# A fused attention and butterfly-FFN kernel: the first unit's row maxima made in two halves, and sixteen extra matmuls in the head

## Chip, cores and metric

One NeuronCore of a Trainium2 chip. The metric is the device time of one execution in microseconds, as the median of several runs. The engines are TensorE (PE; its weight loads are shown as PEld), VectorE (DVE), ScalarE (ACT), GpSimd (POOL) and SyncE (SP), which here issues every DMA.

## What is computed

One post-norm transformer layer in float32. x is 4 x 1024 x 128; there are 16 heads of 64.

```python
q, k, v = (einsum('BSE,EHK->BSHK', x, w) for w in (w_q, w_k, w_v))
logits = einsum('BSHK,BMHK->BSHM', q, k) / sqrt(64)
probs = softmax(logits + causal_mask, axis=3)
att = einsum('BSHK,EHK->BSE', einsum('BSHM,BMHK->BSHK', probs, v), w_o)
x = layernorm(x + att)
h = butterfly(x @ W_exp + b_exp, up_weights)            # 9 stages over 512 features
y = butterfly(gelu(h + up_bias), down_weights) @ W_con + b_con + down_bias
x = layernorm(x + y)
```

The softmax subtracts each row's maximum, so a query row's maximum over its keys must be known before its probabilities are made.

## The kernel before

**Units, steps, places.** The attention is cut into 32 units, one for each batch and pair of heads (`UNITS`). A unit has 1024 queries in two chunks of 512 and 1024 keys in tiles of 128. `STEPS` lists its 12 steps (query chunk, key tile) under the causal mask: steps 0 to 3 are chunk 0 with tiles 0 to 3, steps 4 to 11 chunk 1 with tiles 0 to 7. `window(u)` on TensorE runs the steps in order. In each, `scores` makes two products for each of the two heads, one of the high parts of Q and K (L692) and one of `KH1` by `QL` (L696). `QL` has the low part of Q in its first 64 partitions and, in partition 64, the row of negated maxima, which meets a one in `KH1`: the maximum is subtracted by the matmul. `fill` puts other work ("fillers") at three places of a step: BETWEEN the heads, BEHIND the second head and LATE, which is behind the probability-value products (`pv`, L717). Those run in blocks: behind step 1 the last five of the unit before, behind step 8 those of steps 0 to 3, behind step 9 those of steps 4 to 6.

**Fillers.** `FILL` lists them by step and place. They work for the next unit: the four projections `("proj", n, c)` (n 0 is Q, n 1 is K; c the chunk of tokens), the two V pieces, and the 21 maxima `MAXES` (L631). A maximum multiplies 128 queries of one head by up to 512 keys and VectorE reduces the product (`tensor_tensor_reduce` with the mask at L991, `tensor_reduce` at L994). The first six of `MAXES` are all of query chunk 0 (`CHUNK0_MAXES`); the other 15 are chunk 1. Each filler writes one of four PSUM banks (`WORK`), in turn, and waits until the filler four before it has been read.

**Behind a projection.** ScalarE copies the high part out (L797, two instructions), VectorE subtracts for the low part (L929, two instructions), and SP copies halves between partitions (`copies`, L396 for Q, L400 for K). The first maximum of each chunk waits for both projections' splits and for the copies.

**Behind the last maximum.** In `consume`, VectorE reduces and negates (`NEGM`, L998) and transposes it in four instructions (`NROW`, L1004); SP moves the row into `QL` (`rows`, L408), and the first L696 product of the unit waits for it (`m_landed`).

**The head.** Before unit 0, `PREFETCH` runs for it: projections, V pieces, all 21 maxima, and the first projection of unit 1. Meanwhile GpSimd sends the bias row through the butterfly (L190, L192, L494); for the last two stages it needs a transfer of SP's (L429, `BROW`). Then it starts on masks (L504) and on the sums of probabilities (L518 to L528). SP works through one written order: inputs, `copies(0)`, the loads of w_o, W_con and the biases, `BROW`, W_exp and the next tokens, `rows(0)`, and then for each unit `copies(u + 1)` and `rows(u + 1)`. Every wait in it holds what is behind.

**Weights of the next units.** `stage_low` (Q and K weights) and `stage_v_low` (V weights) on VectorE subtract high parts, both inputs in SBUF (L929, WST and WSV).

Of the kernel before, what the change touches and what calls it, by code (L numbers as in the profile page):

```python
# [24 lines left out]
F32 = mybir.dt.float32  # L25
# [22 lines left out]
NS = len(STEPS)  # L48
# [53 lines left out]
FILLERS = [(s, place, f) for s in range(NS) for place in range(3) for f in FILL[s][place]]  # L102
EARLY = ("proj", 0, 0)
# [9 lines left out]
NWORK, BLK = 4, 32  # L113
LAY_UNITS = TILES // 2
# [15 lines left out]

def unit_fillers(u):

    b, n = u // PAIRS, u % PAIRS
    rows = []
    for s, place, f in FILLERS:
# [12 lines left out]
    rows += [(s, place, f) for f, (unit, s, place) in X1_AT.items() if unit == u]  # L148
    rows += [(s, place, f) for f, (unit, s, place) in ONCE_AT.items() if unit == u]
    if b < B - 1 and n < LAY_UNITS:  # L150
        rows.append(LAY_AT + (("lay", b + 1, n),))
    return sorted(rows, key=lambda row: row[:2])


PREFETCH = [("proj", 0, 0), ("v", 0), ("proj", 1, 0), ("proj", 0, 1), ("v", 1), ("proj", 1, 1)] + MAXES + [("proj", 0, 0)]
# [39 lines left out]
def post_norm_layer(nc, x, w_q, w_k, w_v, w_o, W_exp, b_exp, up_w, up_b, down_w, W_con, b_con, down_b, out):  # L195
    ctx = ExitStack()
    with ctx:
# [156 lines left out]

        block = ctx.enter_context(nc.Block())
# [3 lines left out]
        def _(sp):  # L359
# [42 lines left out]

            def rows(unit):

                par = unit % 2
                sp.wait_ge(nrow_made, (unit + 1))
                dst = QL[K:K + 1, par, :, :].rearrange("a h (t c) -> a (h t) c", t=TILES)
                sp.dma_start(dst.bitcast(F32), NROW[0:2 * TILES, :].bitcast(F32)).then_inc(m_landed, 16)  # L408
# [14 lines left out]
            sp.sem_inc(sums_landed, 16)  # L423
            sp.dma_start(wo_nat, w_o.rearrange("e h k -> e (h k)")).then_inc(in_wo, 16)
# [7 lines left out]
            rows(0)  # L432
# [14 lines left out]
            sp.wait_ge(m_landed, 16 * UNITS)  # L447
# [129 lines left out]
        def _(pe):  # L577
# [20 lines left out]
            def filler(u, f, at):  # L598
# [21 lines left out]
                elif f[0] == "max":  # L620
                    pieces = f[1]
                    unit, nxt = u + 1, (u + 1) % 2
# [60 lines left out]
            def scores(unit, s):  # L683
# [3 lines left out]
                for h in range(2):  # L687
# [6 lines left out]
                    if s == 0 and h == 0:  # L694
                        pe.wait_ge(m_landed, (unit + 1) * 16)
# [99 lines left out]
        def _(act):  # L795
# [123 lines left out]
        def _(dve):  # L919
# [40 lines left out]
            def consume(u, f, at):  # L960
# [19 lines left out]
                elif f[0] == "max":  # L980
                    pieces = f[1]
# [14 lines left out]
                    if f == MAXES[-1]:  # L996
# [191 lines left out]
```

## Time and profile before

| | |
|---|---|
| median of 3 runs | 1035.09 us (1034.93 to 1035.8) |
| the profiled execution | 1035.9 us, span 1034.2 us |
| TensorE busy | 1007.0 us (97% of the span) |
| VectorE, GpSimd, ScalarE busy | 778.0, 750.9, 613.1 us |
| mean granted clock of TensorE | 0.993 |
| first 26 us, first slice of 40 | PE 6 tenths, clock 8 tenths |

All times in the rows are microseconds from the start of the span, and durations are microseconds unless marked ns. A timeline row gives start, duration, engine, line, operation, output<-input, and shapes; "x4" is a group of four in a row, and the bracket at the end is the idle time before it and what ended it. A matmul's duration holds its way through the array; the distance between starts shows what it occupies. The granted clock is a share of 2.4 GHz.

### The profile page before, as it was taken

How to read it: one execution, taken by the hardware profiler on the slowest of the kernel's cores; microseconds unless marked ns; L12 is line 12 of the kernel's file. 1: busy time of each engine (PE TensorE's matmuls, PEld its weight loads, DVE VectorE, ACT ScalarE, POOL GpSimd, SP SyncE). 2: the span in 40 equal slices, each digit the busy share in tenths (PEclk: the TensorE clock that was granted, in tenths of full speed). 3: DMA queues.
4: the chain of work that ended last, by engine and by line, in shares of the span. 5: the costliest groups of instructions: out<-in, count | busy, mean ns of one | idle time of the engine just before them, and what ended most of it. 6: DMA issues, size and time to landing. Idle time of an engine off the chain costs nothing.

```text
span 1034.2 us, 17742 instructions
## 1 busy us (share of the span) xinstructions
PE 1007.0 (97%) x5816; PEld 697.7 (67%) x5816; DVE 778.0 (75%) x2112; ACT 613.1 (59%) x1246; POOL 750.9 (73%) x715
## 2 busy tenths in 40 slices
PE   6799999999999999999999999999999999999997
PEld 4566676676666776676666766767666766765687
DVE  7767777877777777878788778877778888785356
ACT  3555656566656656666556656666555656665544
POOL 6567887777768887777778877777778887777510
PEclk8899999999999999999999999999999999999999
DMA  6233122233222222232232222332222222320002
GB/s 190 62 83 82 45 72 53 62 83 83 58 68 62 63 65 60 63 83 63 70 76 58 62 56 55 83 83 63 66 60 74 63 57 57 83 64 22 22 11 73
DMA packets 48602, 68.71 MB, mean 66 GB/s; under 512 B 15191, under 2 KB 25083, under 8 KB 48510
## 3 DMA queue, kind: packets, MB, share of 16 engines
q1 hardware_dynamic: 48510, 67.57, 25.3%
q8 instruction: 47, 0.77, 0.3%
q14 instruction: 45, 0.37, 0.1%
HBM read 31.11 MB, written 2.36 MB: 32 GB/s over the span
## 4 chain that ended last, share of the span: by engine, by line
PE 92%; DVE 3%; DMA 2%; ACT 1%; issue 1%; POOL 0%; SPq 0%; POOLq 0%; ACTq 0%
PE O L717 25%; PE WORK L631 14%; PE SC L692 14%; PE SC L696 13%; PE WORK L644 6%; PE WORK L679 3%; PE WORK L607 3%; PE WORK L609 3%; PE WORK L608 3%; PE WORK L772 2%; PE WORK L617 1%; PE WORK L619 1%; PE WORK L618 1%; DVE WORK L991 1%; DMA R<-RROW 1%
## 5 line engine op out<-in xcount | busy, mean ns | idle before, releaser
L863 ACT ACTIVATE PR<-SC 128x512 f32<-128x512 f32 (+3 forms) x768 | 352.3, 490 | 263.9 <-PE SC L696 231.4
L519 POOL TENSOR_TENSOR SUM<-SUM,PR 128x1024 f32<-128x1024 f32 (+3 forms) x256 | 419.0, 1637 | 14.8 <-POOL SUM L528 0.5
L991 DVE CUSTOM_DVE_ANT_0 WORK<-WORK,CMASK 128x128 f32<-128x128 f32 (+3 forms) x512 | 239.3, 514 | 65.7 <-PE WORK L631 65.6
L692 PE MATMUL SC<-QH,KHL 128*128 128x512 f32 (+3 forms) x768 | 268.8, 356 | 3.1 <-ACT PR L863 3.0
L696 PE MATMUL SC<-QL,KH 128*128 128x512 f32 (+3 forms) x768 | 261.7, 346 | 3.3 <-DMA QL<-NROW 3.3
L504 POOL TENSOR_SCALAR_AFFINE_SELECT PR<-PR 128x256 f32<-128x256 f32 x256 | 105.9, 415 | 198.0 <-ACT PR L863 197.9
L631 PE MATMUL WORK<-KHL,QH 128*128 128x512 f32 (+3 forms) x768 | 226.5, 365 | 5.9 <-DMA KH<-KHL 4.1
L717 PE MATMUL O<-PR,VLO 128*64 128x512 f32 (+3 forms) x1024 | 200.0, 522 | 0.3 <-DVE OT L1075 0.3
L692 PEld LDWEIGHTS SC<-QH,KHL 128*128 128x128 f32 x768 | 145.2, 189 | 60.7 <-ACT PR L863 28.5
L631 PEld LDWEIGHTS WORK<-KHL,QH 128*128 128x128 f32 x768 | 136.7, 191 | 59.3 <-issue 35.4
L994 DVE TENSOR_REDUCE MP<-WORK 128x1 f32<-128x512 f32 x256 | 164.1, 684 | 4.8
L696 PEld LDWEIGHTS SC<-QL,KH 128*128 128x128 f32 x768 | 145.4, 189 | 14.2 <-DMA QL<-NROW 3.7
L929 DVE TENSOR_TENSOR QL<-WORK,QH 64x512 fp32r<-64x512 f32 x128 | 88.0, 687 | 86.7 <-ACT QH L797 85.5
L528 POOL TENSOR_TENSOR SUM<-PR 128x768 f32<-128x768 f32 x64 | 135.9, 2124 | 1.4 <-ACT PR L863 1.4
L717 PEld LDWEIGHTS O<-PR,VLO 128*64 128x64 f32 x1024 | 64.9, 136 | 104.4 <-issue 77.0
L929 DVE TENSOR_TENSOR KHL<-WORK,KHL 64x512 fp32r<-64x512 f32 x128 | 88.1, 689 | 34.2 <-ACT KHL L797 32.1
L797 ACT ACTIVATE QH<-WORK 64x512 fp32r<-64x512 f32 (+1 forms) x132 | 78.0, 591 | 26.2 <-PE WORK L609 22.6
L797 ACT ACTIVATE KHL<-WORK 64x512 fp32r<-64x512 f32 x128 | 75.7, 592 | 5.0 <-PE WORK L609 1.4
L717 PE MATMUL O<-PR,VHI 128*64 128x256 f32 (+3 forms) x512 | 74.3, 432 | 0.0
L991 DVE DVE_READ_ACCUMULATOR2_ANT MP<- 128x1 f32 x512 | 72.3, 141 | 0.0
L717 PEld LDWEIGHTS O<-PR,VHI 128*64 128x64 f32 x512 | 36.8, 137 | 52.6 <-issue 46.6
L644 PE MATMUL WORK<-WOT,OT 128*128 128x128 f32 x512 | 63.8, 278 | 0.6 <-DVE OT L1075 0.6
(132 smaller groups left out, 1099.0 us busy)
## 6 DMA issues: line engine op xcount, KB each, us to landing
QH<-QH SPq DMA_DIRECT2D x128, 128.0 KB, 2.4
KH<-KHL SPq DMA_DIRECT2D x128, 128.0 KB, 2.3
R<-RROW SPq DMA_DIRECT2D x64, 256.0 KB, 3.8
SW<-in_L_ffn_up_weights_dram SPq DMA_DIRECT2D x9, 512.0 KB, 4.4
SW<-_L_ffn_down_weights_dram SPq DMA_DIRECT2D x9, 512.0 KB, 4.3
out_dram<-X SPq DMA_DIRECT2D x7, 256.0 KB, 2.3
X<-in_L_attn_x_BSE_dram SPq DMA_DIRECT2D x3, 512.0 KB, 4.5
X<-in_L_attn_x_BSE_dram SPq DMA_DIRECT2D x2, 256.0 KB, 3.3
```

The lines of the kernel that those rows point to most:

```text
L519: nc.gpsimd.tensor_tensor(total, total, prob(unit, s), ALU.add).then_inc(add_done, 1)
L528: nc.gpsimd.tensor_tensor(total, first[:, :, START[s]:], prob(unit, s), ALU.add).then_inc(add_done, 1)
L631: t = nc.tensor.matmul(w[:, at_col:at_col + n], QH[:, nxt, h, qt * P:(qt + 1) * P], KHL[:, nxt, h, lo:lo + n], start=True, stop=True)
L644: t = nc.tensor.matmul(w[:, k * P:(k + 1) * P], attended(pair, qc)[:, k * P:(k + 1) * P], WOT[:, pair % PAIRS, :], start=pair < last, stop ...
L692: nc.tensor.matmul(dst, KHL[:, par, h, kt * P:(kt + 1) * P], QH[:, par, h, q0:q0 + n], start=True, stop=False)
L696: nc.tensor.matmul(dst, KH1[:, par, h, kt * P:(kt + 1) * P], QL[:, par, h, q0:q0 + n], start=False, stop=True).then_inc(scores_ready, 1)
L717: t = nc.tensor.matmul(O[qc][h * K:(h + 1) * K, START[s]:], values(unit, kt)[:, h * K:(h + 1) * K], p[:, h, :], start=kt == 0, stop=s == L ...
L797: return nc.scalar.activation(dst, src, ACT.Copy)
L863: nc.scalar.activation(prob(unit, s)[:, h, :], SC[use % NSC][:, 0:n], ACT.Exp, scale=K ** -0.5).then_inc(exp_done, 1)
L929: return nc.vector.tensor_tensor(dst, src, hi_part.bitcast(F32), ALU.subtract)
L991: op = nc.vector.tensor_tensor_reduce(cols, cols, CMASK[:, CH - n:], 1.0, LOWEST, ALU.add, ALU.max, cell)
L994: op = nc.vector.tensor_reduce(cell, cols, AX_X, ALU.max)
```

## The change

1. The head makes unit 0's maxima only up to the tenth: the six of chunk 0, and four of chunk 1 (`FIRST[6:10]`). The eleven others are fillers in steps 0 to 3 of unit 0. They need new lists for unit 0 (`FIRST_FILL`), in which unit 1's projections come in steps 3 and 4 and its maxima in steps 4 to 10 (now 1 to 9).
2. Unit 0's row is made and moved in two halves. Behind the sixth maximum VectorE reduces, negates and transposes once, behind the last a second time; SP moves each half in two transfers (`first_rows`). The first product of step 0 waits for the first half, that of step 4 for the second.
3. On SP `first_rows(0)` stands ahead of the loads of w_o, W_con and the biases; `first_rows(1)` stands where `rows(0)` was.
4. In `PREFETCH` the K projection comes ahead of the first V piece, and the second V piece comes behind the maxima. `stage_low(1)` moves behind the sixth maximum.
5. Sixteen matmuls of 512 columns (`keep_warm`) are added in the head, six behind the last projection and one behind each of ten maxima. They write a score bank that nobody reads.

```diff
+FIRST = [("first", i) for i in range(len(MAXES))]
+WARM_AFTER = {4: 6} | {n: 1 for n in range(5, 15)}
+FIRST_FILL[0] = [FIRST[10:11], FIRST[11:12], []]
+FIRST_FILL[1] = [FIRST[12:13], FIRST[13:15], []]
+FIRST_FILL[2] = [FIRST[15:16], FIRST[16:18], []]
+FIRST_FILL[3] = [FIRST[18:19], FIRST[19:21], [("proj", 1, 0), ("proj", 0, 1)]]
+FIRST_FILL[4] = [[("proj", 1, 1)], [], MAXES[0:1]]
+FIRST_FILL[5] = [[("v", 0)], MAXES[1:3], []]
+FIRST_FILL[6] = [MAXES[3:5], [], [("v", 1)] + MAXES[5:7]]
+FIRST_FILL[7] = [MAXES[7:9], [], MAXES[9:11]]
+FIRST_FILL[8] = [MAXES[11:13], [], MAXES[13:15]]
+FIRST_FILL[9] = [MAXES[15:17], MAXES[17:19], []]
+FIRST_FILL[10] = [MAXES[19:21], [("proj", 0, 0)], []]
...
-PREFETCH = [("proj", 0, 0), ("v", 0), ("proj", 1, 0), ("proj", 0, 1), ("v", 1), ("proj", 1, 1)] + MAXES + [("proj", 0, 0)]
+PREFETCH = [("proj", 0, 0), ("proj", 1, 0), ("v", 0), ("proj", 0, 1), ("proj", 1, 1)] + MAXES[:CHUNK0_MAXES]
+PREFETCH += FIRST[CHUNK0_MAXES:10] + [("v", 1), ("proj", 0, 0)]
...
+            def first_rows(c):
+
+                sp.wait_ge(nrow_made, c + 1)
+                for h in range(2):
+                    dst = QL[K:K + 1, 0, h, c * CH:(c + 1) * CH].rearrange("a (t c) -> a t c", t=TPC)
+                    row = h * TILES + c * TPC
+                    sp.dma_start(dst.bitcast(F32), NROW[row:row + TPC, :].bitcast(F32)).then_inc(m_landed, 16)
...
             copies(0)
             sp.sem_inc(sums_landed, 16)
+            first_rows(0)
             sp.dma_start(wo_nat, w_o.rearrange("e h k -> e (h k)")).then_inc(in_wo, 16)
...
-            rows(0)
+            first_rows(1)
...
-                    if s == 0 and h == 0:
-                        pe.wait_ge(m_landed, (unit + 1) * 16)
+                    if (unit, s, h) == (0, 0, 0):
+                        pe.wait_ge(m_landed, 32)
+                    elif (s, h) == (0, 0) or (unit, s, h) == (0, FIRST_OF[1], 0):
+                        pe.wait_ge(m_landed, rows_landed(unit))
...
+            def keep_warm(times):
+
+                for _ in range(times):
+                    nc.tensor.matmul(SC[0][:, :], XTH[:, 0:P], XTH[:, 0:CH], start=True, stop=True)
...
-                    if f == MAXES[-1]:
+                    if f == MAXES[-1] or (u < 0 and f == MAXES[CHUNK0_MAXES - 1]) or f == ("first", len(MAXES) - 1):
...
-                if f == LAST_PROJ:
+                if f == MAXES[CHUNK0_MAXES - 1]:
                     stage_low(1)
```

## Rows read from the trace of the kernel before

**Rows 1.** Windows: stretch, length, busy us of each engine (instructions), clock, DMA share, GB/s.
```profile
93.50:123.00 29.50, 29.44 (x171) 20.26 (x172) 21.80 (x61) 18.45 (x40) 23.10 (x22) 1.00 0.26 70
```

**Rows 2.** Windows of the head and of unit 0's start, same columns.
```profile
19.00:28.00 9.00, 8.97 (x18) 4.87 (x18) 9.00 (x30) 0.00 (x0) 5.55 (x5) 0.50 0.55 175
33.00:35.60 2.60, 2.60 (x6) 2.06 (x7) 0.00 (x0) 1.19 (x2) 0.24 (x1) 0.50 0.40 92
36.00:38.00 2.00, 1.94 (x10) 1.33 (x8) 0.88 (x2) 1.96 (x5) 0.00 (x0) 1.00 0.00 0
```

**Rows 3.** Timeline of TensorE, the first product with the row.
```profile
32.91 0.80 PE L696 MATMUL SC<-QL,KH 128*128 128x512 f32 x1 [3.26 <-DMA QL<-NROW]
```

**Rows 4.** Timeline of ScalarE, the first copy out of a projection.
```profile
9.19 1.19 ACT L797 ACTIVATE QH<-WORK 64x512 fp32r<-64x512 f32 x2 [1.09 <-PE WORK L609]
```

**Rows 5.** Timeline of VectorE, 15 to 31 us.
```profile
15.84 1.39 DVE L929 TENSOR_TENSOR KHL<-WORK,KHL 64x512 fp32r<-64x512 f32 x2
...
17.97 0.30 DVE L991 CUSTOM_DVE_ANT_0 WORK<-WORK,CMASK 128x128 f32<-128x128 f32 x1
...
21.52 0.33 DVE L991 CUSTOM_DVE_ANT_0 WORK<-WORK,CMASK 128x128 f32<-128x128 f32 x1
...
22.02 2.48 DVE L994 TENSOR_REDUCE MP<-WORK 128x1 f32<-128x512 f32 x4
...
29.96 0.19 DVE L998 TENSOR_REDUCE NEGM<-MP 128x16 f32<-128x32 f32 x1
```

**Rows 6.** Timeline of SP's queue: the first load, and the rows' issues.
```profile
17.05 0.51 SPq L424 DMA_DIRECT2D OT<-in_L_attn_w_o_dram  x1
...
31.05 0.56 SPq L408 DMA_DIRECT2D QL<-NROW  x1
...
37.10 1.10 SPq L400 DMA_DIRECT2D KH<-KHL  x2
...
59.78 0.55 SPq L408 DMA_DIRECT2D QL<-NROW  x1
```

**Rows 7.** Timeline of TensorE, unit 1's first maximum.
```profile
40.06 0.47 PE L631 MATMUL WORK<-KHL,QH 128*128 128x128 f32 x2 [2.12 <-DMA KH<-KHL]
```

**Rows 8.** Timeline of GpSimd, 22 to 51 us.
```profile
22.29 2.28 POOL L192 TENSOR_TENSOR SUM<-R,SUM 1x512 f32<-1x512 f32 x2 [4.04 <-DMA R<-R]
...
29.73 1.25 POOL L494 TENSOR_TENSOR R<-R,W 1x512 f32<-1x512 f32 x1
...
41.63 0.41 POOL L504 TENSOR_SCALAR_AFFINE_SELECT PR<-PR 128x256 f32<-128x256 f32 x1 [3.09 <-ACT PR L863]
...
42.34 1.84 POOL L528 TENSOR_TENSOR SUM<-PR 128x768 f32<-128x768 f32 x1
...
44.71 2.16 POOL L519 TENSOR_TENSOR SUM<-SUM,PR 128x512 f32<-128x512 f32 x2
48.25 2.40 POOL L528 TENSOR_TENSOR SUM<-PR 128x1024 f32<-128x1024 f32 x1 [1.38 <-ACT PR L863]
```

**Rows 9.** Timeline of VectorE in unit 0.
```profile
41.91 0.30 DVE L991 CUSTOM_DVE_ANT_0 WORK<-WORK,CMASK 128x128 f32<-128x128 f32 x1
...
42.51 1.96 DVE L929 TENSOR_TENSOR WST<-WQKV,WST 128x256 fp32r<-128x256 f32 x1
...
47.81 0.41 DVE L929 TENSOR_TENSOR WSV<-WQKV,WSV 128x256 fp32r<-128x256 f32 x1
...
51.26 1.28 DVE L994 TENSOR_REDUCE MP<-WORK 128x1 f32<-128x512 f32 x2
...
57.26 0.69 DVE L991 CUSTOM_DVE_ANT_0 WORK<-WORK,CMASK 128x512 f32<-128x512 f32 x1
```

**Rows 10.** Timeline of TensorE, late unit 0 and the start of unit 1.
```profile
51.94 2.37 PE L717 MATMUL O<-PR,VLO 128*64 128x512 f32 x16
...
60.35 0.38 PE L692 MATMUL SC<-QH,KHL 128*128 128x256 f32 x1
...
63.70 0.39 PE L696 MATMUL SC<-QL,KH 128*128 128x512 f32 x1
```

More of the change, by code:

```diff
@@ L128 @@
 W1_SPLIT_AT = (UNITS - 1, 8)
+FIRST_FILL = [[[], [], []] for _ in range(NS)]
+FIRST_FILL[0] = [FIRST[10:11], FIRST[11:12], []]
[9 more added lines that the diff above has]
+FIRST_FILL[10] = [MAXES[19:21], [("proj", 0, 0)], []]
+FIRST_FILLERS = [(s, place, f) for s in range(NS) for place in range(3) for f in FIRST_FILL[s][place]]
+assert sorted(f for _, _, f in FIRST_FILLERS if f[0] != "first") == sorted(f for _, _, f in FILLERS if f[0] != "norm")
 def unit_fillers(u):
@@ L134, in unit_fillers @@
     rows = []
-    for s, place, f in FILLERS:
+    for s, place, f in FILLERS if u > 0 else FIRST_FILLERS:
         if f[0] == "norm":
@@ L353, in prob, with rows_landed @@
             return PR[:, (unit * NS + s) % PRING, :, 0:n]
+        def rows_landed(unit):
+            return 64 + 16 * unit
         block = ctx.enter_context(nc.Block())
@@ L401, in copies @@
                             .then_inc(dup_landed[c], 16)
+            def first_rows(c):
[4 more added lines that the diff above has]
+                    sp.dma_start(dst.bitcast(F32), NROW[row:row + TPC, :].bitcast(F32)).then_inc(m_landed, 16)
             def rows(unit):
                 par = unit % 2
-                sp.wait_ge(nrow_made, (unit + 1))
+                sp.wait_ge(nrow_made, unit + 2)
                 dst = QL[K:K + 1, par, :, :].rearrange("a h (t c) -> a (h t) c", t=TILES)
@@ L446, in _ @@
             inverses(UNITS - 1)
-            sp.wait_ge(m_landed, 16 * UNITS)
+            sp.wait_ge(m_landed, rows_landed(UNITS - 1))
             for c in range(CHUNKS):
@@ L619, in filler @@
                         t = nc.tensor.matmul(out, XTL[:, lo:lo + P], WSV[:, 0, :], start=False, stop=True)
-                elif f[0] == "max":
-                    pieces = f[1]
-                    unit, nxt = u + 1, (u + 1) % 2
+                elif f[0] in ("max", "first"):
+                    pieces = f[1] if f[0] == "max" else MAXES[f[1]][1]
+                    unit = u + 1 if f[0] == "max" else 0
+                    nxt = unit % 2
+                    if f == ("first", CHUNK0_MAXES):
+                        evacuated(NUMBER[-1, ("proj", 0, 1)])
+                        evacuated(NUMBER[-1, ("proj", 1, 1)])
+                        pe.wait_ge(dup_landed[1], 64)
                     for c in range(CHUNKS):
@@ L738, in _ @@
                 filler(-2 if n == 0 else -1, f, n)
+                keep_warm(WARM_AFTER.get(n, 0))
             for u in range(UNITS):
@@ L823, in evacuate @@
                 w, free = WORK[at % NWORK], work_free[at % NWORK]
-                if f[0] in ("max", "out", "w2", "wo", "con", "bias"):
+                if f[0] in ("max", "first", "out", "w2", "wo", "con", "bias"):
                     return
@@ L979, in consume @@
                     op.then_inc(free, 1)
-                elif f[0] == "max":
-                    pieces = f[1]
+                elif f[0] in ("max", "first"):
+                    pieces = f[1] if f[0] == "max" else MAXES[f[1]][1]
                     dve.wait_ge(work_ready, at + 1)
@@ L995, in consume @@
                     op.then_inc(free, 1)
-                    if f == MAXES[-1]:
+                    if f == MAXES[-1] or (u < 0 and f == MAXES[CHUNK0_MAXES - 1]) or f == ("first", len(MAXES) - 1):
+                        made = 0 if u < 0 else 1 if f[0] == "first" else u + 2
                         dve.wait_ge(free, at // NWORK + 1)
@@ L999, in consume @@
                                                 negate=True).then_inc(negm_made, 1)
-                        dve.wait_ge(negm_made, u + 2)
-                        if u >= 0:
-                            dve.wait_ge(m_landed, (u + 1) * 16)
+                        dve.wait_ge(negm_made, made + 1)
+                        if made == 1:
+                            dve.wait_ge(m_landed, 32)
+                        elif made > 1:
+                            dve.wait_ge(m_landed, rows_landed(u))
                         for b in range(0, P, BLK):
```

## The prediction

> **What bounds the kernel now.** I read the windows of the profile first, then the order of time on each engine for the head (0 to 33 us) and the first unit (33 to 63.7 us). From the third unit on TensorE leaves no hole: 29.44 us busy in a stretch of 29.5 us [rows 1]. So the 31 later units are a block that moves as a whole, and this change is worth what it moves one event, the first row correction of unit 1 on TensorE, now at 63.70 us [rows 10]. Ahead of that the head is a chain without slack on VectorE: the last projection is split at 15.84 us, the maxima run from 17.97 us, the negated maxima stand at 29.96 us, and TensorE, which has waited 3.26 us, gets the row at 32.91 us [rows 3, 5]. In the first unit both engines work, VectorE through 21 maxima for unit 1, TensorE through the scores.
>
> Names: F0 to F20 are the maxima of unit 0 (F0 to F5 chunk 0), M0 to M20 those of unit 1, PV the block of probability-value products behind step 8.
>
> **Part one: the first row comes early.** ScalarE starts copying projections at 9.19 us, 1.19 us for a pair, so 0.6 us for one copy [rows 4]. With the second V piece moved back it copies Q, K, V, Q, K without a gap: 9.19 + 4 x 1.2 + 0.6 = 14.6 us. VectorE's splits cost 1.39 us each and follow one another with 0.03 us between; the last starts at 14.85 us in place of 15.84 us and ends at 16.25 us [rows 5]. The next weights' subtraction, which fills the time from 17.23 to 17.97 us, is now behind F5. F0 starts at 16.3 us. F0 to F5 take 21.52 - 17.97 = 3.55 us, the negated maxima up to the row's issue 31.05 - 29.96 = 1.09 us [rows 5, 6]: row issued at 20.95 us. It is now two transfers, so the second is issued 0.56 us later; landing adds 32.91 - 31.05 = 1.86 us [rows 3, 6]: 23.4 us. That is 9.5 us earlier than now.
>
> **Part two: what is moved into steps 0 to 3.** VectorE goes on with the subtraction (0.42 us while GpSimd stands still, as the V weights' one of the same size [rows 9]), F6 (0.5 us) and F7 to F9 (2.48 / 4 = 0.62 us each [rows 5]): 23.75 us. Unit 1's first projection can only be written when F7 has left its bank (22.5 us); behind the V piece its products end at 23.6 us, ScalarE copies until 24.8 us, VectorE splits until 26.25 us. F10 to F20 take, with the transposes, 31.05 - 23.88 = 7.17 us (F10 starts three reductions behind 22.02 us) [rows 5, 6]. TensorE feeds them without a hole, since steps 0 to 3 hold small scores. Second row issued at 33.4 us, landed 33.4 + 0.56 + 1.86 = 35.8 us. So step 4 starts at about 35.9 us. Nine microseconds are won at the first row, and most are given back here, because the 11 maxima are the same work at the same price and only steps 0 to 3 are hidden behind them.
>
> **Part three: what waits for the second row.** Three things stand behind it. First, TensorE idles. Its last work ahead of step 4, two projections for unit 1, takes the banks of F17 and F18, which VectorE leaves at 30.7 and 31.3 us; it is at step 4 at about 32.3 us and waits 3.6 us. In the trace it idled 3.26 us and then worked at a granted clock of 0.50, the 1.2 GHz level, back at 1.00 (2.4 GHz) by 36 us [rows 2, 3]. So I take half clock for the first 3 us, where a 512-column product costs 2.6 / 6 = 0.43 us [rows 2]. Second, the projection (1, 1) for unit 1 stands between the two heads of step 4. Row correction and three products at 0.43 us, with the last one's drain, end at 37.8 us, ScalarE copies to 39.05 us, VectorE splits to 40.5 us, where M0 starts; now it starts at 41.91 us [rows 9]. Third, SP holds unit 1's copies behind the second row's wait: rows issued until 34.5 us, Q copies 1.15 us, K copies issued at 35.65 us and, as now from 37.10 to 40.06 us, 2.96 us to landing [rows 6, 7]: 38.6 us. This is hidden behind the split.
>
> **Part four: SP and GpSimd.** SP waits for the first row ahead of the loads, that is until 22.05 us in place of 17.05 us [rows 6]; the bias row's move is among them. GpSimd stood waiting for just that move before 22.29 us [rows 8], so its whole bias chain moves by 5 us, from 30.98 to 36.0 us. Then it has a backlog: three masks and a copy at 0.4 us, the add of 1.84 us, a mask, two adds in 2.16 us, then 2.40 us each [rows 8]. The adds end at 39.3, 41.85, 44.25 and 46.65 us. PV needs mask 3 (39.7 us) at 49 us, so no product waits. But VectorE does: the weights' subtraction took 1.96 us beside GpSimd's add of 42.34 us, where the like one took 0.41 us at 47.81 us with GpSimd idle [rows 8, 9]. After the change it is asked for at 41.1 us and ends at 42.2 us (0.65 us lost), and the V weights' one at 45.5 us, ending at 46.95 us (1.05 us lost; bounds 0 and the 2.40 us of a whole add). The row shows the wait; the Trainium skill, page "SBUF — State Buffer", section "Who interferes with whom", has the rule: a VectorE instruction with two SBUF inputs and a GpSimd instruction that reads SBUF take turns, the second fully blocked. This case's 1.96 us agrees. By the rule the backlog works against the change; were VectorE never blocked, the time would be that of the second case below.
>
> **The sum for unit 0.** M0 to the start of M13 is 51.26 - 41.91 = 9.35 us, of which 1.54 us are today's block, so 7.8 us net [rows 9]. 40.5 + 7.8 + 0.65 + 1.05 = 50.0 us. M8 is done 2.0 us before. M12's product takes M8's bank; scores of step 8 and PV follow 0.8 to 0.9 us later: PV at 48.9 us in place of 51.94 us [rows 10]. From PV to step 10 is 60.35 - 51.94 = 8.41 us [rows 10], 8.47 us with two larger maxima. M19 and M20 are now in step 10, behind the second block of products: 0.24 us for a score, 0.43 us for M19's product, 59.78 - 57.26 = 2.52 us to the row's issue [rows 6, 9], 1.86 us to landing, in all 13.5 us behind PV. Unit 1's row is there at 62.4 us. TensorE and ScalarE by themselves would be there 63.70 - 60.35 = 3.35 us behind step 10, with 0.5 us for two more maxima, at 61.2 us; so the row comes last by 1.2 us. 63.70 - 62.4 = 1.3 us gained.
>
> **Warming products.** Sixteen, at 0.22 to 0.43 us, in a stretch in which VectorE sets the pace at 0.5 to 0.64 us per maximum. With them TensorE is busy most of that time, and I count them at zero. Without full clock the projection and V piece ahead of F10 would cost 1.2 us more; the bound on both sides is -1.2 to +0.2 us.
>
> The profiled execution has a span of 1034.2 us and 1035.9 us in all; the runs' median is 1035.09 us, 0.8 us under it. 1.3 us off gives a span of 1032.9 us and a median of 1033.8 us.
>
> **Rivals.** *Forecast, 0.46*: the row of unit 1 sets the end of unit 0; 1033.8 us, on its own 1033.1 to 1034.9 us.
> *Faster, 0.30*: GpSimd's instructions leave gaps where VectorE needs them, and the clock stays up across the second row's wait. M0 at 39.7 us, M13 at 47.5 us and M8 done at 45.5 us; then TensorE's own work sets PV. From the K copies (38.6 us) it has M0 to M12 (5376 columns), two V pieces (3072) and the scores of steps 5 to 8 (8192), 32.5 slots of 512 columns at half of 0.43 us, 7.5 us with gaps, then 0.3 us to PV at 46.4 us; row at 59.9 us: 3.8 us gained, 1031.3 us. With one of the two alone it is 1.5 to 2.4 us. For it: GpSimd's adds lie back to back only if the probabilities come in time, and any hole lets VectorE in. Against it: the backlog of part four.
> *No gain, 0.14*: the warming products don't hold the clock. The second row comes 1.2 us later, part of the blocks falls away; 1034.9 us.
> *Slower, 0.10*: half clock persists behind the second row. In the head it stayed at 0.50 over 9 us with TensorE paced by VectorE [rows 2]. The 7.5 us of work become 15 us, PV at 53.9 us, row at 67.4 us: 3.7 us lost, 1038.8 us. It decides against the change from PV later than 50.2 us on, that is from half clock for over 7 us beyond 38.6 us. Against it: at half clock TensorE is the slow engine and has few holes.
>
> **The numbers.** What a measurement can tell from no change is about 0.2%, 2.1 us. The faster case lies beyond it and a little of the forecast's tail (0.32 in all), the forecast and the third case within it (0.58), the last beyond it on the other side (0.10). The range runs from the faster case, 1031.3 us, to between the third and the last, 1036.4 us.
>
> **What the profile would show.** Right: first row correction at 23.5 to 25 us; bias chain on GpSimd ending near 36 us; TensorE idle about 3.5 us ahead of step 4 with a clock of 0.50 behind it; M0 at 40 to 41 us; a subtraction of over 1 us; PV near 49 us; TensorE waiting for unit 1's row at 62 to 63 us. Wrong: the second row far from 35.8 us, unit 1 waiting for ScalarE as now, PV before 47.5 us or behind 50.2 us, or units 2 to 31 of another length.

## The result, and the profile after

| | before | after |
|---|---|---|
| median, same chip, 7 runs each | 1035.38 us (1034.93 to 1036.07) | 1039.22 us (1037.01 to 1040.57) |
| ratio to before, 95% interval | | 1.0033 (1.0022 to 1.0044) |
| the profiled execution | 1035.9 us, span 1034.2 us | 1037.48 us, span 1035.8 us |
| TensorE busy, mean granted clock | 1007.0 us, 0.993 | 1006.0 us, 0.998 |

The kernel became 3.8 us slower where 1.3 us of gain were forecast. The head went as planned; the loss came later. Below are lines of the page of after, in which VectorE and GpSimd do what they did before, while TensorE's clock is nearly always up:

```profile
span 1035.8 us, 17783 instructions
...
PE 1006.0 (97%) x5832; PEld 698.3 (67%) x5832; DVE 779.1 (75%) x2117; ACT 613.9 (59%) x1246; POOL 750.5 (72%) x715
...
PE   6799999999999999999999999999999999999997
...
PEclk9999999999999999999999999999999999999999
```

The timeline of TensorE (start, duration, engine, line, operation, in brackets the idle time before it and what ended it) has the two row products of unit 0 and, from step 4 to unit 1's start, every stop of 0.2 us or more. L735 is the product with the row, L668 a maximum's, L729 a score's first product, L756 PV:

```profile
23.64 0.40 PE L735 MATMUL SC<-QL,KH 128*128 128x512 f32 x1
...
35.90 0.50 PE L735 MATMUL SC<-QL,KH 128*128 128x512 f32 x1 [3.35 <-DMA QL<-NROW]
...
39.17 0.47 PE L668 MATMUL WORK<-KHL,QH 128*128 128x128 f32 x2 [1.62 <-DMA KH<-KHL]
...
48.23 0.38 PE L668 MATMUL WORK<-KHL,QH 128*128 128x256 f32 x1 [1.76 <-DVE MP L1039]
...
48.82 0.39 PE L668 MATMUL WORK<-KHL,QH 128*128 128x256 f32 x1 [0.21 <-DVE MP L1039]
...
49.60 2.37 PE L756 MATMUL O<-PR,VLO 128*64 128x512 f32 x16
...
61.74 0.49 PE L729 MATMUL SC<-QH,KHL 128*128 128x512 f32 x1 [0.75 <-ACT PR L908]
...
63.54 0.50 PE L735 MATMUL SC<-QL,KH 128*128 128x512 f32 x1 [1.31 <-DMA QL<-NROW]
```

The first row's product is at 23.64 us (before 32.91 [rows 3]), the second's at 35.90, and unit 1's at 63.54 us (before 63.70 [rows 10]): nine microseconds are won and 0.16 are left. The timeline of VectorE shows where the middle went:

```profile
16.02 0.30 DVE L1036 CUSTOM_DVE_ANT_0 WORK<-WORK,CMASK 128x128 f32<-128x128 f32 x1
...
20.84 0.42 DVE L974 TENSOR_TENSOR WST<-WQKV,WST 128x256 fp32r<-128x256 f32 x1
...
38.35 1.39 DVE L974 TENSOR_TENSOR KHL<-WORK,KHL 64x512 fp32r<-64x512 f32 x2 [1.92 <-ACT KHL L842]
39.78 0.30 DVE L1036 CUSTOM_DVE_ANT_0 WORK<-WORK,CMASK 128x128 f32<-128x128 f32 x1
...
40.37 0.95 DVE L974 TENSOR_TENSOR WST<-WQKV,WST 128x256 fp32r<-128x256 f32 x1
...
45.10 2.47 DVE L974 TENSOR_TENSOR WSV<-WQKV,WSV 128x256 fp32r<-128x256 f32 x1
...
52.45 1.29 DVE L1039 TENSOR_REDUCE MP<-WORK 128x1 f32<-128x512 f32 x2 [1.71 <-PE WORK L668]
```

The V weights' subtraction (L974, WSV) takes 2.47 us in the midst of unit 1's maxima; before it took 0.41 [rows 9]. TensorE's 1.76 us of waiting at 48.23 us stand behind it. The timeline of GpSimd shows what ran beside it:

```profile
34.97 1.26 POOL L526 TENSOR_TENSOR R<-R,W 1x512 f32<-1x512 f32 x1
36.19 1.12 POOL L536 TENSOR_SCALAR_AFFINE_SELECT PR<-PR 128x256 f32<-128x256 f32 x3
...
42.01 2.40 POOL L560 TENSOR_TENSOR SUM<-PR 128x1024 f32<-128x1024 f32 x1
44.91 2.38 POOL L551 TENSOR_TENSOR SUM<-SUM,PR 128x1024 f32<-128x1024 f32 x1 [0.50 <-POOL SUM L560]
```

VectorE asked at 45.10 us, 0.19 us behind the start of an add that ended at 47.29, and was done at 47.57.

The windows around unit 1's start (length, busy us of PE, PEld, DVE, ACT and POOL with instructions, granted clock, DMA share, GB/s) show what follows the two waits there:

```profile
60.00:64.00 4.00, 1.94 (x12) 1.45 (x11) 3.60 (x10) 1.63 (x4) 3.81 (x5) 1.00 0.11 37
65.00:68.00 3.00, 3.00 (x10) 2.61 (x9) 1.27 (x2) 2.22 (x5) 0.66 (x2) 0.50 0.46 127
69.00:93.50 24.50, 24.42 (x145) 15.91 (x141) 19.31 (x56) 12.94 (x27) 18.53 (x16) 1.00 0.27 67
```

TensorE did 1.94 us of work in 4, then had work without a hole at half the clock, and is back at 1.00 behind 68.1 us. From unit 1's row product to the issue of unit 2's row it is 28.46 us (63.54 to 92.00); before it was 27.26 (63.70 to 90.96). The issues on SP's queue, first after, then before:

```profile
92.00 0.56 SPq L439 DMA_DIRECT2D QL<-NROW  x1
```
```profile
90.96 0.56 SPq L408 DMA_DIRECT2D QL<-NROW  x1
```

So the row of unit 2 is 1.04 us late. Of the later rows unit 24's is 0.55 us late, the last unit's 2.39, and the span is 1.6 us longer.

### The profile page after: what moved, and what is told of

Same layout as the page of the kernel before. It is cut to its first block, busy times and chain, and to the rows that moved or that the text cites. A ratio compares the mean times of both kernels' runs of the same rounds, so it can differ in the third digit from the quotient of the medians.

```text
span 1035.8 us, 17783 instructions
## 1 busy us (share of the span) xinstructions
PE 1006.0 (97%) x5832; PEld 698.3 (67%) x5832; DVE 779.1 (75%) x2117; ACT 613.9 (59%) x1246; POOL 750.5 (72%) x715
## 4 chain that ended last, share of the span: by engine, by line
PE 89%; DVE 4%; DMA 4%; ACT 1%; issue 1%; SPq 1%; POOL 1%; POOLq 0%; ACTq 0%; DVEq 0%
PE O L756 25%; PE WORK L668 13%; PE SC L729 12%; PE SC L735 12%; PE WORK L681 5%; PE WORK L716 3%; PE WORK L639 3%; PE WORK L641 3%; PE WORK L640 3%; PE WORK L817 2%; DMA R<-RROW 2%; DVE WORK L1036 2%; PE WORK L649 1%; PE WORK L651 1%; PE WORK L650 1%; DMA RROW<-RCOL 1%
## 5 line engine op out<-in xcount | busy, mean ns | idle before, releaser
L729 PE MATMUL SC<-QH,KHL 128*128 128x512 f32 (+3 forms) x768 | 269.0, 356 | 3.7 <-ACT PR L908 3.7
L735 PE MATMUL SC<-QL,KH 128*128 128x512 f32 (+3 forms) x768 | 261.7, 346 | 4.7 <-DMA QL<-NROW 4.7
L668 PE MATMUL WORK<-KHL,QH 128*128 128x512 f32 (+3 forms) x768 | 224.1, 358 | 5.4 <-DMA KH<-KHL 2.9
L756 PE MATMUL O<-PR,VLO 128*64 128x512 f32 (+3 forms) x1024 | 199.9, 522 | 1.5 <-DVE OT L1123 1.5
L729 PEld LDWEIGHTS SC<-QH,KHL 128*128 128x128 f32 x768 | 145.2, 189 | 61.1 <-ACT PR L908 28.9
L668 PEld LDWEIGHTS WORK<-KHL,QH 128*128 128x128 f32 x768 | 135.0, 189 | 56.5 <-issue 34.2
L735 PEld LDWEIGHTS SC<-QL,KH 128*128 128x128 f32 x768 | 145.4, 189 | 15.9 <-DMA QL<-NROW 5.4
L974 DVE TENSOR_TENSOR QL<-WORK,QH 64x512 fp32r<-64x512 f32 x128 | 88.0, 688 | 85.1 <-ACT QH L842 84.0
L756 PEld LDWEIGHTS O<-PR,VLO 128*64 128x64 f32 x1024 | 64.9, 136 | 105.7 <-issue 78.9
L974 DVE TENSOR_TENSOR KHL<-WORK,KHL 64x512 fp32r<-64x512 f32 x128 | 88.2, 689 | 34.9 <-ACT KHL L842 32.8
L756 PE MATMUL O<-PR,VHI 128*64 128x256 f32 (+3 forms) x512 | 74.3, 432 | 0.0
L756 PEld LDWEIGHTS O<-PR,VHI 128*64 128x64 f32 x512 | 36.8, 137 | 52.6 <-issue 46.6
```

Source lines behind the costliest of these rows:

```text
L668: t = nc.tensor.matmul(w[:, at_col:at_col + n], QH[:, nxt, h, qt * P:(qt + 1) * P], KHL[:, nxt, h, lo:lo + n], start=True, stop=True)
L729: nc.tensor.matmul(dst, KHL[:, par, h, kt * P:(kt + 1) * P], QH[:, par, h, q0:q0 + n], start=True, stop=False)
L735: nc.tensor.matmul(dst, KH1[:, par, h, kt * P:(kt + 1) * P], QL[:, par, h, q0:q0 + n], start=False, stop=True).then_inc(scores_ready, 1)
L756: t = nc.tensor.matmul(O[qc][h * K:(h + 1) * K, START[s]:], values(unit, kt)[:, h * K:(h + 1) * K], p[:, h, :], start=kt == 0, stop=s == L ...
L974: return nc.vector.tensor_tensor(dst, src, hi_part.bitcast(F32), ALU.subtract)
```

## The experiments

No experiment leaves out a part of the computation. Several add products of 512 columns whose results nobody reads (`keep_warm`); like the sixteen of the change they are extra work. Medians are in microseconds, the ratio is to the kernel before on the same chip, with its 95% interval. Not all kernels ran on one chip, so two of them are compared by their ratios, where 0.001 is 1.04 us.

**The same kernel again**, to see how executions differ. No edit.

> The changed kernel once more, for a second trace and more spans. In its first trace unit 1 began 0.16 us earlier than before (63.54 against 63.70 us), then the granted clock stood at 0.50 from 64.9 to 68.1 us and unit 2's row was issued 1.04 us later than before. Theory CLOCK: the loss is made of stretches at 1.2 GHz behind TensorE's waits (3.35 us ahead of step 4, 1.3 us at unit 1's row), which fall differently in each execution. Then spans spread over 3 us as the mean clock does (0.993 to 0.998), and this trace has its half-clock stretches in other places than the first or of other length. Theory SCHEDULE: the later row and the waits cost the time by themselves; then the half-clock stretches are as in the first trace, median 1038 to 1040 us either way.

Measured: 1039.37 (1037.37 to 1040.08), ratio 1.0035 (1.0021 to 1.0048). The execution profiled was one of 1040.08 us. Two things tell it from the first: its head is 0.7 us later (first row issued at 21.51 us for 20.84), and its clock falls. Windows of it:

```profile
36.00:39.00 3.00, 2.42 (x6) 1.82 (x6) 1.10 (x2) 0.91 (x2) 3.00 (x6) 0.51 0.68 158
39.00:43.00 4.00, 3.65 (x21) 2.92 (x20) 3.04 (x8) 3.60 (x8) 3.82 (x5) 0.94 0.72 165
...
49.00:52.00 3.00, 2.77 (x8) 1.30 (x10) 2.54 (x7) 0.60 (x1) 0.19 (x1) 0.62 0.00 0
52.00:56.00 4.00, 4.00 (x25) 2.32 (x22) 1.16 (x2) 0.71 (x2) 2.54 (x2) 0.86 0.00 0
```

and its waits on TensorE:

```profile
36.58 0.79 PE L735 MATMUL SC<-QL,KH 128*128 128x512 f32 x1 [3.37 <-DMA QL<-NROW]
...
49.02 0.39 PE L668 MATMUL WORK<-KHL,QH 128*128 128x256 f32 x1 [1.53 <-DVE MP L1039]
...
65.92 0.50 PE L735 MATMUL SC<-QL,KH 128*128 128x512 f32 x1 [1.28 <-DMA QL<-NROW]
```

The first profiled execution of after had 1.00 in all four windows. Here the clock is at 0.50 behind the wait for the second row (36.0 to 39.5 us), again behind the wait for VectorE (49.7 to 53.2 us), and a third time in unit 1 (66.7 to 70.2 us). Unit 1's row product is 2.38 us later (65.92 for 63.54), of which 0.68 us were there at the second row's product (36.58 for 35.90), ahead of any cost of the clock; the whole execution is 2.6 us longer.

**Without the sixteen products of the head; and they alone in the kernel before.**

```diff
-WARM_AFTER = {4: 6} | {n: 1 for n in range(5, 15)}
+WARM_AFTER = {}
```

> The change without its sixteen extra matmuls. CLOCK: without them the head runs at 1.2 GHz behind 18 us, as before the change; the projection ahead of the eleventh maximum and so the second row come about 1.2 us later, which takes away nothing or 1 us; but the chip's state behind the head is that of the kernel before, so the half-clock stretch could move from unit 1 into the head and step 4: 1036 to 1038 us, with mean clock 0.985 to 0.993. SCHEDULE: 1.2 us later rows, 1039 to 1041 us.

> The kernel before with sixteen unread matmuls in the head, six behind its last projection and one behind each of its first ten maxima. CLOCK: the clock stays up to 24 us, then falls; unit 0 starts with the same row at 31 to 33 us, the time is the same, 1035 us. PLACE OF THE CODE: from unit 2 on the units in which the reciprocals' way through DRAM takes over 2 us (367, 513, 630, 688, 776, 805, 921 us in the kernel before) move to others, as in the change (193, 281, 631, 747, 777, 865, 923 us), and TensorE's waits for them with it (0.2 to 0.3 us in the kernel before, 1.5 to 2.5 us in the change): up to 1 us slower. If these waits are chance, the list is as in the kernel before and 1035.0 us.

Measured: 1038.17 (1037.77 to 1040.83), ratio 1.0033 (1.002 to 1.0045); and 1035.5 (1034.23 to 1036.75), ratio 1.0003 (0.9995 to 1.0012). Without them the clock is at 0.50 from 16.1 to 26.3 us and the second row's product at 38.08 us, 2.2 us later than in after, but the median is no worse. So what the products buy in the head is lost again behind it, and they don't cause the loss. This trace has no half clock behind 26.3 us, and still issues unit 2's row at 93.50 us, 2.5 us later than before: a late second row loses time without the clock too. In the kernel before they change nothing that can be measured.

**Filling TensorE's waits.** Fourteen unread products ahead of step 4 and seven ahead of unit 1's first score; then each alone.

```diff
                     pe.wait_ge(exp_done, unit * 2 * NS + use + 1)
+                    keep_warm({(0, 4, 0): 14, (1, 0, 0): 7}.get((unit, s, h), 0))
```

> The change with matmuls nobody reads also in TensorE's two waits: fourteen ahead of step 4 of unit 0 and seven ahead of unit 1's first score, both ahead of a product that waits anyway. CLOCK: no stretch at 1.2 GHz behind 12 us, mean clock 0.998 or more in all executions, the spread of spans falls below 1.5 us, and the median comes to 1035 to 1036 us, 3 us under the changed kernel. SCHEDULE: within 0.5 us of the changed kernel.

> The change with fourteen unread matmuls ahead of step 4 of unit 0 only, not ahead of unit 1. CLOCK, in the form that the first long wait (3.35 us) starts the falls: the median comes to 1035 to 1036 us, as with both waits filled (1034.6 us). If the wait at unit 1 is the one that counts: 1038 to 1039.5 us.

> The change with seven unread matmuls ahead of unit 1's first score only. CLOCK at unit 1: no stretch at 0.50 behind 62 us, which costs 1.2 us in unit 1 (28.5 us from its row product to unit 2's row issue in place of 27.3 us). If this fall carries the loss: 1034.6 to 1036 us, as with both waits filled. If each fall is a term of its own: 1037.8 us, 1.2 us under the changed kernel.

Measured: both 1034.57 (1033.74 to 1038.56), ratio 1.0002 (0.9992 to 1.0012); step 4 alone 1039.04 (1038.94 to 1039.72), 1.0044 (1.003 to 1.0057); unit 1 alone 1037.45 (1034.78 to 1039.27), 1.0022 (1.0013 to 1.0032). Both together took the whole loss away, with extra work on an engine that is busy 97% of the time; the interval of the last overlaps that of after (1.0022 to 1.0044). Of the eleven runs with both, seven have spans of 1032.0 to 1033.4 us at mean clocks of 0.997 to 0.999, four of 1035.3 to 1036.8 at 0.995 to 0.997. The parts don't add up: alone, the one at step 4 brings nothing. In its trace the clock stays up at 36 us and falls at 49 us instead, behind the wait for VectorE, and again in unit 1:

```profile
36.00:39.00 3.00, 1.66 (x6) 1.05 (x6) 1.07 (x2) 2.19 (x4) 3.00 (x6) 1.00 0.80 185
...
49.00:52.00 3.00, 2.92 (x7) 1.25 (x9) 2.00 (x7) 0.60 (x1) 0.68 (x2) 0.50 0.00 0
52.00:60.00 8.00, 8.00 (x47) 4.37 (x43) 5.12 (x10) 1.33 (x3) 4.78 (x3) 0.98 0.00 1
64.00:68.00 4.00, 2.73 (x8) 2.25 (x9) 1.48 (x3) 1.51 (x3) 2.70 (x4) 0.75 0.63 190
```

With unit 1's wait alone filled, the trace has no half clock behind 62 us. Not all of what both fills gave need be the clock: behind unit 2's row the trace of both is 1.5 to 2 us shorter than those of one, for another reason (last section).

**Is it the backlog on GpSimd?** The bias row's move goes ahead of the first row, as in the order of before.

```diff
             sp.sem_inc(sums_landed, 16)
+            sp.wait_ge(blocks_done, 1)
+            sp.dma_start(BROW, BLOCKS).then_inc(brow_in, 16)
             first_rows(0)
```

> The change with SP's move of the bias row ahead of the first row's wait (the other loads stay behind it). GpSimd's bias chain, which waited 9.38 us for that move, resumes at about 20.5 us in place of 27.5 us and is through at about 29 us, so it has no backlog in unit 0. BLOCK (the V weights' subtraction, 2.47 us beside an add of GpSimd's, holds up TensorE 1.76 us at 46.5 us): the subtraction takes 0.42 us, the wait is gone, PV starts at about 47.5 us in place of 49.60 us, unit 1's row product is at 61.5 us in place of 63.54 us, and the median falls by 2 us to 1037.2 us; with CLOCK also the half-clock stretch at 49 to 53 us seen in the second trace goes with its wait, 1036 us. If the backlog doesn't matter: 1039 us.

Measured: 1038.72 (1036.99 to 1040.18), ratio 1.0033 (1.0021 to 1.0046). The bias chain ends at 29.0 us, 7 us earlier. GpSimd has no backlog left in unit 0, as its idle 9.20 us show, and still the subtraction is blocked. First GpSimd, then VectorE:

```profile
43.90 2.40 POOL L560 TENSOR_TENSOR SUM<-PR 128x1024 f32<-128x1024 f32 x1 [9.20 <-ACT PR L908]
46.79 2.40 POOL L551 TENSOR_TENSOR SUM<-SUM,PR 128x1024 f32<-128x1024 f32 x1 [0.50 <-POOL SUM L560]
```
```profile
47.59 1.89 DVE L974 TENSOR_TENSOR WSV<-WQKV,WSV 128x256 fp32r<-128x256 f32 x1
```

The first of these adds comes when its probabilities do, and that is about the time when VectorE reduces M6, behind which the subtraction is written. What blocks it is its place in the order, and a backlog of GpSimd isn't needed. My theory of the backlog fell here.

**The subtraction in another place.** In unit 0 it comes behind M10 instead of M6.

```diff
-                        if f == MAXES[6] and u % 2 == 0 and u + 2 < UNITS:
+                        if f == MAXES[6 if u > 0 else 10] and u % 2 == 0 and u + 2 < UNITS:
                             stage_v_low(u + 2)
```

> The change with the V weights' subtraction of unit 0 four maxima later on VectorE, behind M10 in place of M6, where GpSimd has nothing to add. With the bias row first the subtraction was blocked as before (1.89 us), so the backlog is not what blocks it; its place beside the second add is. BLOCK: it takes 0.42 us, TensorE's wait of 1.5 to 1.8 us ahead of M11 goes, PV starts 1.5 to 2 us earlier (47.6 to 48.0 us in a trace whose clock stays up), unit 1's row product follows by as much, median 1037 us. If GpSimd's add catches it again: 1039 us.

Measured: 1036.04 (1034.51 to 1038.02), ratio 1.0011 (1.0002 to 1.002), by the ratios 2.3 us less than after. VectorE, then GpSimd:

```profile
49.17 0.42 DVE L974 TENSOR_TENSOR WSV<-WQKV,WSV 128x256 fp32r<-128x256 f32 x1
```
```profile
46.31 2.40 POOL L551 TENSOR_TENSOR SUM<-SUM,PR 128x1024 f32<-128x1024 f32 x1 [0.50 <-POOL SUM L560]
49.77 0.41 POOL L536 TENSOR_SCALAR_AFFINE_SELECT PR<-PR 128x256 f32<-128x256 f32 x1 [1.07 <-ACT PR L908]
```

It falls into GpSimd's gap and takes 0.42 us; TensorE's wait at 48 us is gone, and this trace has no fall of the clock near 49 us. The 2 us of one instruction were worth 2.3 us, and the interval lies below that of after.

**The last two maxima.** M19 and M20 stand in step 9, ahead of the block of products, where the maxima ended before. Then the same with fourteen products at step 4, and with both fills and the bias row first.

```diff
-FIRST_FILL[9] = [MAXES[15:17], MAXES[17:19], []]
-FIRST_FILL[10] = [MAXES[19:21], [("proj", 0, 0)], []]
+FIRST_FILL[9] = [MAXES[15:17], MAXES[17:21], []]
+FIRST_FILL[10] = [[], [("proj", 0, 0)], []]
```

> The change with unit 1's last two maxima in step 9 of unit 0, ahead of the block of probability-value products, as in the kernel before, in place of step 10. CLOCK: VectorE has unit 1's row about 2 us earlier (issued at 59.5 in place of 61.67 us), TensorE's wait at unit 1 shrinks from 1.8 us to nothing (only ScalarE's 0.75 us stays, start at 62 us), so half clock behind it becomes rare; 1036 to 1037 us. SCHEDULE: the row alone is worth its 1.5 us: 1037.5 us. If neither the wait nor the row matters, 1039 us.

> The change with unit 1's last two maxima in step 9 and fourteen unread matmuls ahead of step 4. The last maxima alone gave 1036.7 us, the filled waits 1034.6 us. If the row and the clock are two terms that add: 1033 us, with unit 1's scores at 61 us and no half clock between 36 and 40 us. If both work on the same microseconds: 1034.5 to 1035 us.

> The change with three edits at once: the bias row's move ahead of the first row's wait, unit 1's last two maxima in step 9, and unread matmuls in the waits ahead of step 4 and of unit 1. If the three causes (GpSimd's backlog, the late row, the clock) stand beside each other: unit 1 starts at 59 to 60 us in place of 63.5 us, the clock stays up behind 20 us, and the median is 1031.5 to 1033 us, 2 to 3.5 us under the kernel before. If the clock alone was the cause: as with the filled waits, 1034.6 us.

Measured: 1036.66 (1034.54 to 1038.19), ratio 1.0016 (1.0007 to 1.0025); 1034.93 (1033.0 to 1037.27), 1.0005 (0.9996 to 1.0014); 1037.74 (1035.53 to 1039.04), 1.0023 (1.0013 to 1.0034). The row of unit 1 is issued at 57.56 us for 61.67, and TensorE waits there for ScalarE only:

```profile
61.19 0.49 PE L729 MATMUL SC<-QH,KHL 128*128 128x512 f32 x1 [0.75 <-ACT PR L908]
```

This trace helped itself to a second gain: the subtraction, at 46.02 us, began just ahead of an add of 46.14 us and took 0.41 us, so what this trace gained (it is of the fastest of the eleven executions) is not the late maxima's alone. By the ratios the edit gained 1.8 us, with intervals that overlap a little. In the third kernel the seven products ahead of unit 1 fill a wait that is no longer there; 1.89 us of them lie on the path, although the clock of this trace is 1.00 from the head on. A filler is worth nothing where the wait is gone.

**The kernel before with its wait filled.** Fourteen unread products ahead of its first product with the row.

> The kernel before with fourteen unread matmuls ahead of unit 0's first score, where TensorE waits 3.26 us for the row. CLOCK: the 2.6 us at 0.50 behind that wait (33 to 35.6 us) go; the first three steps and unit 1's first K projection end 0.8 to 1.3 us earlier, and with them the first maximum; 1034.3 us, 1 us under the kernel before. If the clock behind this wait is hidden by VectorE and SP's copies: 1035.2 us.

> The kernel before once more, for a second trace. CLOCK: its half-clock stretches are again in the head's maxima (about 18 to 29 us, where VectorE sets the pace) and in some executions behind the row's wait, but none behind 40 us; unit 1's row product at 63.0 to 63.8 us, unit 2's row issued at 90.5 to 91 us.

Measured: 1034.16 (1033.08 to 1035.14), ratio 0.9987 (0.9979 to 0.9996). The kernel before pays for its wait too, but 1.3 us. A further execution of before (1034.85 us) has half clock from 16.4 to 26.8 us, where VectorE sets the pace, and from 30.1 to 37.0 us, around the row's wait and in the first steps behind it; its V subtraction is unblocked (0.41 us) and unit 1's rows leave at 58.91 us.

**All of it retimed.** Bias row first, late maxima early, subtraction behind M10, and two more: the projection (1, 1) in step 3, ahead of the wait for the second row, and unit 1's first Q copies on SP ahead of that wait; eleven unread products at step 4. Then this without those eleven, and without the head's sixteen.

```diff
+FIRST_FILL[3] = [FIRST[18:19], FIRST[19:21], [("proj", 1, 0), ("proj", 0, 1), ("proj", 1, 1)]]
+FIRST_FILL[4] = [[], [], MAXES[0:1]]
...
+            copies(1, range(1))
             first_rows(1)
...
+                    keep_warm({(0, 4, 0): 11}.get((unit, s, h), 0))
```

> The change with all waits that the traces name taken away: the bias row's move first, unit 1's second K projection in step 3 (no longer between the heads of step 4), the Q copies of unit 1 ahead of the second row's wait on SP, the V weights' subtraction behind M10, the last two maxima in step 9, eleven unread matmuls ahead of step 4. M0 starts at 38 us in place of 39.8 us, PV at 45 to 46 us in place of 49.6 us, unit 1's first scores at 57.5 to 58.5 us in place of 63.5 us; median 1030 to 1032 us, under both kernels. If the two-halves scheme itself costs what it gains: 1034 to 1035 us.

> The retimed kernel without the eleven unread matmuls ahead of step 4. CLOCK: the wait of 3.4 us is open again and the clock stands at 0.50 for 3 us or more behind 36 us in most executions; M0 comes 0.5 to 1 us later and the median is 1032.3 to 1033.3 us. If the fall is hidden as long as nothing behind it waits: 1031.8 us.

> The retimed kernel without the sixteen unread matmuls of the head, with those ahead of step 4. CLOCK: the head's maxima at 0.50, the V piece and the projection behind them 1.2 to 1.5 us later, as in the change without them (second row issued at 35.8 us in place of 33.6 us there); the whole of unit 0 is later by that: 1033.3 us. If VectorE's order hides it: 1031.8 us.

Measured: 1031.77 (1031.01 to 1032.79), ratio 0.9971 (0.9961 to 0.9982); 1034.39 (1033.43 to 1035.75), 0.9994 (0.9986 to 1.0003); 1032.33 (1031.08 to 1033.43), 0.9975 (0.9967 to 0.9984). The first beats before by 3.1 us, and after, by the ratios, by 6.4. TensorE's stops in it:

```profile
36.38 0.50 PE L739 MATMUL SC<-QL,KH 128*128 128x512 f32 x1 [0.28 <-DMA QL<-NROW]
...
38.37 0.47 PE L671 MATMUL WORK<-KHL,QH 128*128 128x128 f32 x2 [1.02 <-DMA KH<-KHL]
...
59.14 0.49 PE L733 MATMUL SC<-QH,KHL 128*128 128x512 f32 x1 [0.75 <-ACT PR L912]
```

Unit 1 starts at 59.14 us in place of 61.74, its row has been issued since 55.51, and the clock is 1.00 behind step 4. Leaving the wait ahead of step 4 open costs 2.4 us of this, and here the clock stands alone: both traces have the second row's product at 36.38 us and differ behind it by half clock from 36.0 to 42.9 us in the open one; unit 1 starts at 61.19 us for 59.14, and from unit 2's row on both take 943.2 us. The sixteen of the head make a difference of 0.4 us (the intervals overlap), although the clock is at 0.50 from 15.1 to 25.3 us without them.

## Why the prediction was wrong

**Part one, right.** F0 started at 16.02 us (16.3 forecast), the first row's product at 23.64 (23.4).

**Part two, right.** F10 began at 26.25 us (26.25), the second row was issued at 33.61 (33.4) and used at 35.90 (35.9). The 3.35 us of idling are the 3.6 of the working.

**Part three, half right.** M0 started at 39.78 us, 0.7 earlier than forecast, with the clock up in the profiled execution; in the second one it was at 0.51 and M0 came at 41.3 us, 0.7 us of it from the later head. The step took this for the only place of half clock in unit 0. That was wrong, see below.

**Part four: the mechanism right, its size and its cause wrong.** The bias chain ended at 36.2 us (36.0), no product waited for a mask, and both subtractions were blocked. The weights' one at 20.84 us, with GpSimd waiting, took the 0.42 us counted; the one at 40.37 took 0.95 for 0.42 + 0.65. The V weights' took 2.47 us where 0.42 + 1.05 were counted: the forecast laid GpSimd's adds back to back and had the last of them end at 46.65 us; it ended at 47.29. So 2.05 us were lost for 1.05, near the upper bound of a whole add (2.40). And the backlog, to which I put it down, is not needed for it (bias row first: 1.89 us, idle GpSimd). The exclusion is what the Trainium skill says in page "SBUF — State Buffer", section "Who interferes with whom": a VectorE instruction with both inputs in SBUF and a GpSimd instruction that reads SBUF shut each other out. The runs agree: 2.47 us (after), 1.89 (bias row first) and 2.09 (second trace of after) beside an add, in each until 0.28 or 0.29 us behind the add's end, and 0.41 and 0.42 in a gap.

**The sum for unit 0, 1.1 us off.** PV was at 49.60 us (48.9), and from PV to the row's product it took 13.94 us (13.5): 63.54 for 62.4. That the row of unit 1 sets the end was right, the wait of 1.31 us (1.2 forecast) too.

**The step that failed: the clock behind short waits.** The prediction priced half clock once, for 3 us behind the second row, and took units 2 to 31 for a block. The profiled execution, with its clock up through all of unit 0, still lost about 1.2 us at half clock in unit 1, behind waits of 0.75 and 1.31 us. For comparison, the stretch from unit 1's row product to unit 2's row: 28.46, 28.50, 28.51 and 28.49 us in the four traces in which the clock falls there (both of after, subtraction later, step 4 filled), 27.32 and 27.75 where the same two waits are followed by no fall (bias row first, no warming products), 27.26 before. The other 0.6 us were lost to waits of another kind in later units (last section). So its 1.6 us of loss and the 1.3 of gain that were forecast differ by 1.1 (unit 0), 1.2 (the clock in unit 1) and 0.6: together 2.9.

Most executions lose more. The median of after lies 1.7 us above its profiled execution, where I took it 0.8 us below, and that makes up the other 2.5 us between the 1033.8 us forecast and the 1039.2 measured. The trace of the second execution is 2.4 us later at unit 1's row, 0.7 us from its head and the rest with half clock at 36 and at 49 us. The kernel before has the lower mean clock (0.993), but most of its half clock lies in the head, where VectorE sets the pace. The change took it out there and made holes of 1.3 to 3.4 us in a stretch in which TensorE is the bound.

That the holes bring the falls shows over all traces of the changed kernel and its variants. With the second row's wait open (2.79 to 3.38 us) the clock fell there in six of eight traces; with the wait filled in none of six. With the wait for unit 1's row open it fell in four of six, without it in none of eight. What a fall of some 7 us costs in unit 0 is the difference of the two retimed kernels, 2.05 us in the traces.

**The rivals.** *Slower* had the right sign, and in the profiled execution not the form: the clock stayed up behind the second row and fell behind a later wait. In three other traces (bias row first, subtraction later, unit 1 filled) it was down for 6.8 us, to 43.1 or 44.3 us, short of the 45.6 from which that case was to decide; PV came at 51.51 us in the first of them and at 50.93 in the second trace of after, both behind the 50.2 us that were its sign. *Faster* describes what the retimed kernel does: no block, clock up, unit 1's row hidden. It was forecast at 1031.3 us and this one took 1031.8, but it took six edits to get there. *No gain* was wrong for its reason: the sixteen products do hold the clock in the head, and it hardly matters; without them the second row came 2.2 us later (1.2 forecast), and the median was 1038.2 us, not 1034.9.

**The terms overlap.** By the ratios against after: subtraction moved 2.3 us, maxima early 1.8, both waits filled 3.2, unit 1's alone 1.1 (not clear of noise), step 4's alone none; all retimed 6.4. Each schedule wait removed is also an occasion less for the clock to fall, so no split of the loss into clock and schedule is unique. And the mean clock doesn't explain every difference: with maxima early and step 4 filled, spans run from 1031.3 to 1034.5 us at 0.999. What makes that is open, and so is why one execution's clock falls behind a wait and the next one's doesn't.

## What to carry to other kernels

Before moving work off a path, list the holes that the move makes in the engine that is the bound afterwards: a hole of 2.8 us cost 2.4 us in clock behind it in the retimed kernel, two of 0.75 and 1.3 us some 0.7 to 1.2 us in unit 1, and so a change that shortens one long way and makes four waits can lose. Close such holes by order first (an instruction one place earlier, a transfer ahead of the wait that holds its queue) and with unread products only where a hole is left. A VectorE instruction that reads two SBUF inputs wants a place in which GpSimd is known to stand still; look at where its adds start, not at how long its queue is. And where a variant changes more than the edit meant, compare stretches of the trace as well as totals.

## What was not expected of the hardware

**The clock after the same wait.** A wait of 3.35 us ahead of step 4 left the clock at 1.00 in one execution of after; 3.37 us were followed by 0.51 in the next one. Waits of 1.5 to 1.8 us near 48 us were followed by a fall at 49 us in three traces (the second of after, step 4 filled, both filled) and by none in four (the first of after, no warming products, maxima early with step 4 filled, and that with the bias row first and both fills); 0.75 and 1.3 us, with little work between, by one in four traces and by none in two. Falls lasted from 3.5 to 6.9 us in unit 0.

**A small transfer that is late in some units.** For the reciprocals of every unit SP sends 8 KB (`RROW` from `RCOL`) and waits for them. It mostly takes 1.4 us, in some units 1.6 to 3.7. In the one of after that costs most, at 747.24 us, the DMA view of just that stretch has a packet of an instruction queue in it; the view's lines are queue, packets, MB and share, then the issues with the time to landing:

```profile
q1 hardware_dynamic: 144, 0.01, 3.4%
q14 instruction: 1, 0.01, 0.7%
issues: line engine op xcount, KB each, median us to landing
R<-RROW SPq DMA_DIRECT2D x1, 256.0 KB, 3.4
RROW<-RCOL SPq DMA_DIRECT2D x1, 8.0 KB, 2.6
```

Before, in the same unit (746.68 us), there is no such packet and it takes 1.4 us. TensorE feels it behind:

```profile
755.70 0.65 PE L756 MATMUL O<-PR,VLO 128*64 128x512 f32 x2 [0.93 <-DVE OT L1123]
```

Such waits come to 0.9 us in before, 0.58 of them in the last unit (behind a transfer of 3.7 us):

```profile
983.66 3.81 PE L644 MATMUL WORK<-WOT,OT 128*128 128x128 f32 x32 [0.58 <-DVE OT L1075]
```

They come to 0.6 us in its second trace and to 1.5 and 2.5 in the two of after, in the same units both times. So a kernel with other code has them in other units. One run bears this out: with the sixteen products in the head of before, the slow transfer at 367 us is gone (1.4 us) and there is one of 2.7 us at 191 us, with such a packet, where after has one at 193; those at 512, 629, 688, 775, 804 and 920 us stay. In the two traces of after, this one and the first of before, 27 of the 29 transfers over 1.55 us have such a packet in their stretch, and 6 of the 99 others. That the packets delay the transfer is still argued from this.

These waits are on the path. After loses 1.35 us between unit 2's row and the last unit's, with 1.2 us more of them there, and gets 0.8 back behind it, where the 0.58 us of before lie. Over all eighteen traces the time from unit 2's row to the end follows them: 941.8 to 942.8 us in the five with 0.3 to 0.7 us of waits, 942.5 to 943.8 in the eight with 0.9 to 1.7, and 943.4 to 944.1 in the five with 2.0 to 2.5. Both waits filled has 0.3 us of them and 941.9 us, step 4 alone 2.0 and 943.4, unit 1 alone 2.2 and 943.9; that can be most of the 2.1 us by which the parts fell short of the whole. The retimed kernel has 1.7 us of them and is still the fastest.
